# Decoder layer on one Trainium2 core: another order of DVE's and SP's work in the cross-attention stage

## The reference, cut to what matters

```
x1 = layernorm(x  + mixer(x))
x2 = layernorm(x1 + cross_attention(x1, context))
     # cross: softmax over 77 keys, 16 heads of 32, causal mask on key <= token
o  = slots + attention(slots, x2, x2)      # 16 slots per sequence look at all its tokens
o  = o + expert_e(layernorm(o_e))          # slot e through expert e
y  = layernorm(x2 + attention(x2, o, o))
```

## Time and profile before

| | |
|---|---|
| three timed runs | 1517.11, 1521.77, 1521.76 us, median 1521.76 |
| profiled execution | 1513.52 us, its span 1511.8 us |
| busy, share of the span | PE 1315.2 us (87%), DVE 788.5 (52%), ACT 442.9 (29%), POOL 219.1 (14%) |
| mean granted TensorE clock | 0.946 of full speed |
| chain that ended last | PE 45%, DMA 23%, DVE 19%, ACT 5%, issue 3% |
| cross stage, 750 to 800 us | PE busy 45.09 of 50 us, DVE 42.57, ACT 19.98, POOL 11.39; DMA share 0.70 |
| expert stage, 950 to 1000 us | PE busy 45.11 of 50 us, DVE 3.58; DMA share 1.00 |

### The profile page before, as it was taken

One profiled execution on the slowest core, in us unless ns is written; L12 is line 12 of the kernel. 1 busy time (PEld: TensorE's weight loads), 2 busy tenths in 40 slices (PEclk: granted clock), 3 DMA queues, 4 the chain that ended last, 5 costly groups with the idle time before them and its releaser, 6 DMA issues.

```text
span 1511.8 us, 25784 instructions
## 1 busy us (share of the span) xinstructions
PE 1315.2 (87%) x10085; PEld 768.2 (51%) x10085; DVE 788.5 (52%) x1450; ACT 442.9 (29%) x1158; POOL 219.1 (14%) x182
## 2 busy tenths in 40 slices
PE   7899999999989898988989888886766776679998
PEld 4777777777756565656666555221111111126554
DVE  1656567666787888888888863100000000004665
ACT  2434444444235333333333331000000000002444
POOL 1122221022131212122222210000000000001221
PEclk9999999999999999999999999988887778889999
DMA  9453344344467887767777778999999999995673
GB/s 339 162 148 94 82 119 117 86 119 116 116 188 217 243 260 210 221 192 227 202 222 207 206 240 309 416 419 423 428 427 424 427 427 427 423 423 178 200 235 125
DMA packets 133925, 379.71 MB, mean 251 GB/s; under 512 B 15739, under 2 KB 53243, under 8 KB 116680
## 3 DMA queue, kind: packets, MB, share of 16 engines
q1 hardware_dynamic: 129032, 363.77, 69.5%
q10 hardware_dynamic: 4800, 14.68, 2.6%
HBM read 311.03 MB, written 67.37 MB: 250 GB/s over the span
## 4 chain that ended last, share of the span: by engine, by line
PE 45%; DMA 23%; DVE 19%; ACT 5%; issue 3%; SPq 0%; POOL 0%; DVEq 0%; ACTq 0%; POOLq 0%
DMA all_ring<-in_e_Wg 21%; PE mxw_bank L184 10%; PE mix_scores L730 7%; PE mix_scores L1714 4%; PE mxw_bank L2198 4%; PE mxw_bank L1060 4%; DVE all_space L1169 4%; DVE all_more L1154 3%; DVE all_space L1140 3%; DVE all_more L1138 3%; DVE all_more L1145 3%; ACT all_space L1081 2%; PE mix_scores L2231 2%; PE mxw_bank L2231 2%; PE mix_scores L1737 2%
## 5 line engine op out<-in xcount | busy, mean ns | idle before, releaser
L1714 PE MATMUL mix_scores<-all_ring,all_space 128*32 128x512 f32 x968 | 148.0, 706 | 80.0 <-DMA all_ring<-in_e_Wg 42.8
L1764 DVE TENSOR_TENSOR all_space<-all_space 128x512 f32<-128x512 f32 x16 | 11.1, 694 | 377.6 <-ACT all_space L1773 377.6
L184 PE MATMUL mxw_bank<-all_ring,all_space 128*128 128x256 f32 x768 | 176.9, 384 | 1.6 <-DMA all_space<-in_WinT 1.6
L184 PEld LDWEIGHTS mxw_bank<-all_ring,all_space 128*128 128x128 f32 x768 | 143.4, 190 | 32.3 <-issue 10.8
L1773 ACT ACTIVATE all_space<-mix_scores 128x512 f32<-128x512 f32 x32 | 19.1, 597 | 406.6 <-PE mix_scores L1723 406.6
L254 DVE SCALAR_TENSOR_TENSOR all_ring<-all_ring,all_space 128x256 f32<-128x256 f32 x192 | 84.4, 482 | 75.0 <-ACT all_ring L203 72.7
L1714 PEld LDWEIGHTS mix_scores<-all_ring,all_space 128*32 128x32 f32 x968 | 31.0, 118 | 179.8 <-DMA all_ring<-in_e_Wg 71.6
L1737 PE MATMUL mix_scores<-all_ring,all_space 128*32 128x512 f32 x480 | 113.2, 745 | 10.2 <-DVE all_space L1767 10.2
L1014 PE MATMUL mxw_bank<-all_space 128*128 128x512 f32 x248 | 113.8, 602 | 6.3 <-ACT all_space L1126 6.3
L1233 POOL TENSOR_TENSOR all_space<-all_space,all_more 128x1232 f32<-128x1232 f32 x32 | 72.5, 2267 | 290.4 <-DVE all_more L1148 290.4
L730 PE MATMUL mix_scores<-all_space,all_ring 128*128 128x512 f32 x240 | 105.4, 592 | 0.0
(11 more groups left out here) (312 smaller groups left out, 2092.2 us busy)
## 6 DMA issues: line engine op xcount, KB each, us to landing
all_ring<-in_e_W SPq DMA_DIRECT2D x55, 2048.0 KB, 24.8
all_ring<-in_e_Wg SPq DMA_DIRECT2D x28, 2048.0 KB, 26.2
scratch_probs<-all_more SPq DMA_DIRECT2D x32, 768.0 KB, 3.3
all_space<-scratch_probs SPq DMA_DIRECT2D x64, 256.0 KB
all_ring<-in_xT SPq DMA_DIRECT2D x8, 1024.0 KB, 9.3
all_ring<-scratch_rates SPq DMA_DIRECT2D x64, 128.0 KB, 4.6
all_z<-in_x SPq DMA_DIRECT2D x16, 512.0 KB, 5.3
scratch_x1T<-all_more SPq DMA_DIRECT2D x128, 64.0 KB, 1.8
```

Of the source, the lines that this page charges most:

```text
L184: last = nc.tensor.matmul(bank[:, i * BT:(i + 1) * BT], hold["win"][:, k, m * P:(m + 1) * P], hold["xT"][b % 2][:, k, :], start=(k == 0), ...
L1714: last = nc.tensor.matmul(bank[w][q * ROWS:(q + 1) * ROWS, :], hm[u][:, k, :], weights[k % 2][:, q * FQ:(q + 1) * FQ], start=(k == 0), sto ...
```

## The change

DVE's order in a step: x2 is turned ahead of the scores (in steps 0 and 1 behind them, as before), and the slots' maxima stand between the scores and the denominators. SP stores the probabilities of tile t+1 ahead of x2 of tile t-1. The x1 rows of chunk 13 are turned and stored ahead of step 0: on DVE behind the denominators of tile 0, on SP ahead of the store of tile 0's probabilities. No instruction is added or removed, and none changes its operands.

```diff
-LATE_STORES = {0: CHUNKS - 3, 3: CHUNKS - 2, 4: CHUNKS - 1}
+LATE_STORES = {3: CHUNKS - 2, 4: CHUNKS - 1}
...
             load_x1T(sp, 3, 1)
+            first["store"](sp, CHUNKS - 3)
             store_probs(sp, 0)
...
-                if before(t, 1):
-                    store_x2(sp, t - 1, 1 - u)
                 if ahead(t, 1):
                     store_probs(sp, t + 1)
                 if before(t, 1):
+                    store_x2(sp, t - 1, 1 - u)
                     store_x2T(sp, t - 1)
...
             denominators(dve, 0)
+            first["turn_rows"](dve, CHUNKS - 3)
             first["rate_outputs"](dve, END)
...
-                if ahead(t, 2):
-                    take_scores(dve, t + 2, known(t, CHUNKS - 2))
+                if known(t, *range(EARLY)):
+                    take_scores(dve, t + 2, False)
                 if before(t, 1):
                     turn_x2(dve, t - 1, 1 - u)
+                if ahead(t, 2) and not known(t, *range(EARLY)):
+                    take_scores(dve, t + 2, known(t, CHUNKS - 2))
+                if before(t, 2):
+                    slot_maxima(dve, t - 2, seq(-2))
                 if ahead(t, 2):
                     denominators(dve, t + 2)
                 if before(t, 2):
-                    slot_maxima(dve, t - 2, seq(-2))
                     slot_sums(dve, t - 2, u, seq(-2))
```

## The result

| | before | after |
|---|---|---|
| timed runs | 1520.58 us (1517.11 to 1521.77, 4 runs) | 1482.43 us (1479.86 to 1484.87, 4 runs) |
| ratio | | 0.975, interval 0.973 to 0.978 |
| profiled execution, its span | 1513.52, 1511.8 | 1484.87, 1483.1 |
| PE, DVE busy | 87%, 52% | 89%, 50% |
| chain that ended last | PE 45%, DMA 23%, DVE 19% | PE 63%, DMA 23%, DVE 4% |

By its size this is rival B (1487.5), not the forecast (1502.8). The profiled execution of before was some 7 us under its own timed runs and that of after was not, so the spans differ by 28.7 us only. The traces can account for that part; the rest of the 38 is the distance of single executions.

A forecast was written before the change was run, and what follows sets the result against it. PE's 14.1 us a step was the floor, DVE's detour on top. Gains 14.6 (steady) - 0.4 (step 29) + 3.5 (start) + 1.3 (steps 3, 4) = 19.0 us, giving 1502.8 us; range 1484 to 1516.

The forecast's parts named there:

- rival B: In steady steps L1183 starts before POOL and is not held; PE's 14.15 a step binds: 1487.5 us, chance 0.27.
- (1) the maxima: Steady step on DVE: maxima fill the exponential's gap, removing L1169's 1.9 us and waits of 0.69 and 0.76.
- (2) What is late next: Slots' sums behind the reciprocal: POOL starts first by 0.04, so L1183 is held to POOL's end.
- the two ends: Bounds on the price of holding L1183 behind POOL in a steady step: 0 and 2.1 us.
- A: The forecast itself: L1183 held behind POOL, steady steps of 14.65 us; 1502.8 us in all, chance 0.55.
- (3) The loop over two steps: Late slot scores make DVE wait for PE; a loop through DVE, POOL, ACT and PE gives 14.65 us a step.
- The loss of 0.4 at step 29: At step 29 PE has no queries left and waits for the last scores, which come 0.42 later: 0.4 us lost.
- The start: Steps 1 and 2: chunk 13's earlier turn and stores let probabilities land sooner, gaining 3.5 us, bounds 0 and 7.
- The turn's cover: Before step 0, DVE's 1.81 us wait for PE ahead of L791 hides chunk 13's 1.23 us turn.
- the 2.5 named: Sign at the start: PE's wait before L1004 at step 2 falls under 2.5 us, from 5.52.
- C: The two-step loop has no slack: 15.25 us a step, little but the start gained, 1518 us; chance 0.12.
- D: DVE's new wait for slot scores lengthens each step by 0.5 to 0.6 us: slower, 1532 us, chance 0.06.

The follow-up runs named there:

- e2: The kernel before with only the slots' maxima moved ahead of the denominators: 1490.13 us, ratio 0.981.
- e5: The kernel before with one added wait, so POOL normalises only after DVE has done the slots' maxima: 1491.58 us, ratio 0.983.
- e7: The changed kernel with four one-number memsets directly ahead of L1183, behind the wait for L1181: 1500.45 us, ratio 0.988.
- e1: The changed kernel with one one-number memset between L1181 and the wait for it; L1183's lead over POOL stayed: 1484.66 us, ratio 0.977.
- e3: The kernel before with only x2's turn moved ahead of the scores: 1540.04 us, ratio 1.014.
- e6: The changed kernel with x2 turned behind the scores again, as in the kernel before: 1476.64 us, ratio 0.972.
- e4: The kernel before with only chunk 13 turned and stored sooner and the probabilities stored ahead of x2: 1515.65 us, ratio 0.997.
- second execution: The unaltered changed kernel, timed and profiled again beside the last group of experiments: 1484.83 us, ratio 0.978.
- e8: e6 with probabilities turned ahead of the token additions and PE taking the next tile's scores between L1049 and L1060: 1462.84 us, ratio 0.964.
- e9: e8 with the token additions ahead of the turn of probabilities again, as in the change: 1488.22 us, ratio 0.981.

## Why the prediction was wrong in size and right in kind

**What bounds it, (1) the maxima: right.** L1169 is 0.16 everywhere, the wait of L1181 for ACT and PE's idle time at L1049 are gone from the steady steps, and the maxima alone (e2) are worth 29.6 us. e5 shows without any move on DVE that POOL's operation was the cause.

**(2) What is late next: this step failed.** It gave L1183 a start "some 0.04 later" than POOL from an L1181 of 0.16, and so held it to POOL's end in every step. L1181 began where the forecast put it, 0.16 ahead of POOL, but lasted 0.10 in 25 of 32 tiles, shorter than L1169 or L1183 of the same size. L1183 then leads by 0.02, not POOL by 0.04, and is not held. The 0.16 was read from the earlier trace rows, where L1181 stood behind a wait; in the new place it stands directly behind the reciprocal. The rule the step used, who starts first wins, was right, down to 0.02 on either side. The size was right as well: e7 puts POOL ahead and loses 15.6 us, landing at 1500.45, 18.9 us below before, where the forecast had 19.0. That it agrees to 0.1 is in part luck: in e7's trace steps 5 to 29 gain 14.1 for the forecast's 14.6, and the steps ahead of them 2.4 for 4.8. Only the choice between the two ends was wrong; with a margin of 0.04 built of durations that vary by 0.06, B deserved about as much chance as A.

The race isn't won everywhere. At step 2 the first execution of after lost it (above), and at step 14, where the masked scores make the step longer, L1181 itself waited for ACT, began 0.10 behind POOL and was held to POOL's end in both executions (2.18 and 2.19).

The section "Who interferes with whom" of SBUF — State Buffer in the Trainium skill states that issue order decides. Here e1 and the trace of after, with L1183 0.02 us ahead of POOL by recorded starts, and e7, with it 0.02 behind, agree.

**(3) The loop over two steps: right, but not the bound.** 14.65 was forecast for held sums, e7 shows 14.73. (The forecast multiplied by a gain of 0.65; from its own 15.35 to 14.65 it is 0.70, 1.2 us more over 24 steps.) At step 14, where it took up to 1 us less, the gain was 1.18 (16.71 to 15.53), like the others. Without the hold PE bounds: 14.15 by B, 14.06 to 14.14 measured. The two ends of the price, 0 and 2.1 us a step, were the right ones.

**x2's turn ahead.** Its 0.42 on the scores is 0.38 in e3. In the changed kernel DVE hides it in the wait for L1042, but ACT's copy L1126 comes later for it and costs PE 0.12 a step, 3 us in all, where the forecast had nothing beyond step 29; between the medians it is 6 to 8 (e6). The loss of 0.4 at step 29 isn't shown: it was 15.75 against 15.38 in the first execution, but 14.05 in the second, and 16.54 in e4, whose order there is that of before.

**The start: right in kind, its size within what two executions differ by.** 3.5 was forecast for steps 1 and 2. Alone (e4) the edit gives 3.9 up to step 3 (51.30 us from tile 0's turn, 47.35) and 4.0 in the median. In the two executions of after it is 2.2 and 3.8, both 1.7 up to step 2; the rest depends on how long a sum was held there. In the changed kernel and in e1, which has its order, a hold of 0.54 goes with 16.32 from step 2 to 3, one of 1.74 with 17.52 and one of 2.27 with 18.01. The turn's cover, DVE's wait for PE ahead of L791, went from 1.81 to 0.72:

```profile
414.05 1.19 DVE L805 STREAM_TRANSPOSE all_more<-all_space 128x1024 f32<-128x1024 f32 x1
415.95 1.29 DVE L791 TENSOR_TENSOR all_ring<-mxw_bank,all_ring 128x512 f32<-128x512 f32 x2 [0.72 <-PE mxw_bank L722]
```

PE's wait at step 2 is 2.06, below the 2.5 named. Steps 3 and 4 gained 1.3 together, as said (32.37 to 31.10), and 2.0 in the second execution.

**The range.** In the stage itself B's sum of 34 lies between the two executions of after, 30.6 and 35.6 against the one of before. The 38 between the medians is more than the 28.7 between the spans because the profiled execution of before lay 7.1 below its median and that of after 2.4 above. The forecast took the first offset as fixed and gave it no error. Its low end, 1484, stood 3.5 under B's 1487.5, less than the 4.6 that it calls noise, and the result lies 1.6 below it.

**Rivals.** C (15.25) and D (slower) did not come. D's kind of loss is real, though: e3, x2's turn ahead without the maxima, is 20 us slower, 9 by a longer path through DVE and the rest in stretches where the granted clock was at its lower level.

## What to carry to other kernels

Here tiny DVE operations of two SBUF operands (L1169, L1181, L1183) lasted to the end of the POOL operation that had started ahead of them. Look for such a one by a maximum far above the minimum in one line's durations (2.05 and 0.16 here), and move it, or let POOL wait, whichever is cheaper. Take the duration of a tiny operation from a place like the one it will have. If a plan rests on who starts first within a tenth of a microsecond, count both outcomes as about equally likely, and then fix the order by a wait or an instruction in between. Once the slowest engine is PE, its remaining gap is worth filling only together with the edit that frees what waits behind the work pushed back: e8 and e9 lie 25 us apart. And before a microsecond or two of a single trace is given a cause, read a second execution of the same kernel.

## What the runs showed of the hardware that was not expected

- DVE and POOL decide their order within 0.02 us of recorded start: at 0.02 ahead (after, e1) the DVE operation lasts 0.16, at 0.02 behind (e7, step 2 of after) 2.27, with nothing in between in the rows shown.
- L1181, two numbers a partition, takes 0.10 in 25 tiles of after, 0.14 to 0.16 in six and 2.18 in one, where it is held; before, behind a wait for ACT, it took 0.15 to 0.16 in all 32. A difference of that size decides 15.6 us. All 25 stand directly behind the reciprocal; why it is shorter there isn't known.
- Memsets of one number were recorded in 0.06 beside a held two-operand operation of the same engine; DVE's next instruction began 0.08 us before the recorded end of the one ahead (706.71 + 0.25 against 706.88).
- TensorE's granted clock fell inside steps that looked busy: in e3, with idle times of up to 1.34 and 0.55 a step, L1060 lasted 2.6 to 3.7 in 13 of the 24 steps behind step 5 (granted clock 0.52 over 715.0 to 718.5, and 0.50 is the lower level); with 1.09 and 0.55 it did so in none before and in one of e4.
- The eight matmuls of L1014 last 3.70 when ACT's copy, which they read, ends 0.05 ahead of the first (after), and 3.59 when it ends 0.41 ahead (e6).
